# Gated cross-attention block on one core: ScalarE's exponentials ahead of two copies, the second norm's scaling two slots sooner

## The reference

```python
x = x + tanh(g_xattn) * attention(layernorm(x), ctx, ctx)    # x, ctx: (32, 256, 256) f32, 16 heads of 16
x = x + tanh(g_ffn)   * ffn(layernorm(x))                    # 256 -> 768 -> 256, quantised weights and activations
# attention: q, k, v = y @ W.T + b; rotary embedding of q and k;
#   scores = q k^T / 4, -1e9 where |i - j| > 50; softmax; weighted sum of v; @ Wo.T + bo
# ffn: q(x) -> up, gate; gate * sigmoid(gate); * up; @ w_down.T, each rounded with one scale for the whole tensor
```

## Time and profile before

| | |
|---|---|
| median of 3 runs | 1364.79 us (1361.7 to 1365.65) |
| profiled execution | 1366.92 us, of which the trace spans 1365.2 us |
| attention, one unit of the steady part | 22.35 us |
| busy over the span | PE 1198.0 us, DVE 1200.9 us, ACT 830.6 us, POOL 561.2 us |
| granted TensorE clock, steady part | 1.00 |

### The profile page before, as it was taken

How to read it: one execution, slowest core, us unless ns; L and a number is a source line. 1 busy time by engine, 2 the same in 40 slices (tenths; PEclk the granted TensorE clock), 3 DMA queues, 4 the chain that set the end, 5 groups by cost and what they waited for, 6 DMA issues and landing times. The chain is left out here.

```text
span 1365.2 us, 27834 instructions
## 1 busy us (share of the span) xinstructions
PE 1198.0 (88%) x8995; PEld 790.7 (58%) x8995; DVE 1200.9 (88%) x3603; ACT 830.6 (61%) x1336; POOL 561.2 (41%) x1357
## 2 busy tenths in 40 slices
PE   5789898989898989888898759998999799968998
PEld 3457676767666666666665434443433334427887
DVE  3789999999999999999998749997999989988886
ACT  3256666666666666666665436664677599983332
POOL 1177777777777777787877510000000000000000
PEclk9699999999999999999999769998999999988999
DMA  2636454545545554546462302223455455646765
GB/s 78 170 106 190 132 172 143 162 145 159 159 145 148 156 165 140 172 133 172 137 183 87 102 8 93 116 92 127 163 183 185 157 191 197 199 165 205 244 222 169
DMA packets 132369, 207.27 MB, mean 152 GB/s; under 512 B 11159, under 2 KB 97050, under 8 KB 126106
## 3 DMA queue, kind: packets, MB, share of 16 engines
q1 hardware_dynamic: 132250, 205.86, 47.6%
HBM read 125.60 MB, written 79.69 MB: 150 GB/s over the span
## 5 line engine op out<-in xcount | busy, mean ns | idle before, releaser
L670 DVE CUSTOM_DVE_ANT_0 psum<-psum,band 128x178 f32<-128x178 f32 x1024 | 317.2, 373 | 47.6 <-PE psum L880 47.2
L551 ACT ACTIVATE probs<-psum 128x356 f32<-128x356 f32 x512 | 210.9, 469 | 152.4 <-PE psum L897 152.3
L1090 PE MATMUL psum<-xnT,w_upT 128*128 (+1 forms) x1152 | 261.2, 384 | 18.9 <-DVE maxima L1314 8.8
L485 POOL TENSOR_SCALAR_AFFINE_SELECT probs<-probs 128x154 f32<-128x154 f32 (+1 forms) x512 | 212.2, 431 | 140.8 <-ACT probs L551 138.4
L1090 PEld LDWEIGHTS psum<-xnT,w_upT 128*128 128x128 f16 x1152 | 109.9, 99 | 170.0 <-issue 32.6
L494 POOL TENSOR_SCALAR_AFFINE_SELECT probs<-probs 128x254 f32<-128x254 f32 (+1 forms) x512 | 205.0, 425 | 0.0
L897 PE MATMUL psum<-q_stack,k_stack 98*128 98x178 bf16 x1024 | 133.2, 242 | 35.9 <-ACT probs L551 24.5
L880 PE MATMUL psum<-k_stack,q_stack 96*128 96x178 bf16 x1024 | 136.8, 245 | 24.2 <-DVE smax L670 21.4
L670 DVE DVE_READ_ACCUMULATOR2_ANT smax<- 128x1 f32 x1024 | 142.9, 140 | 0.0
L1690 PE MATMUL psum<-w_downT,xnT 128*128 128x256 f16 x1152 | 128.3, 276 | 15.9 <-DVE xnT L1640 15.9
L1090 PE MATMUL psum<-xnT,w_gateT 128*128 (+1 forms) x576 | 126.5, 383 | 6.9 <-DVE xnT L1163 6.9
(11 more groups left out here) (190 smaller groups left out, 2274.0 us busy)
## 6 DMA issues: line engine op xcount, KB each, us to landing
k_parts_scratch<-k_parts SPq DMA_DIRECT2D x32, 384.0 KB, 2.5
q_parts_scratch<-q_parts SPq DMA_DIRECT2D x32, 384.0 KB, 2.7
k_stack<-k_parts_scratch SPq DMA_DIRECT2D x32, 384.0 KB, 4.1
q_stack<-q_parts_scratch SPq DMA_DIRECT2D x32, 384.0 KB, 4.8
gate_scratch<-g_stage SPq DMA_DIRECT2D x16, 768.0 KB, 3.3
g_in<-gate_scratch SPq DMA_DIRECT2D x16, 768.0 KB, 4.6
sig_scratch<-w_gateT SPq DMA_DIRECT2D x32, 384.0 KB, 2.3
sig_again<-sig_scratch SPq DMA_DIRECT2D x32, 384.0 KB, 3.4
```

What stands on the lines that cost most here:

```text
L485: nc.gpsimd.affine_select(out=t[:, :, 0:n], in_=t[:, :, 0:n], pattern=[[0, 2], [1, n]], compare_op=ALU.is_ge, fill=0.0, base=WINDOW - off, ...
L551: nc.scalar.activation(ring_tile(probs, b, pair, c)[:].rearrange("p e j -> p (e j)"), scoreT_bank[c][:, 0:2 * SPAN], ACT.Exp, scale=DK ** ...
L670: ins = nc.vector.tensor_tensor_reduce(out=mine, in0=mine, in1=keep["band"][:, t, :], scale=1.0, scalar=-3e38, op0=ALU.add, op1=ALU.max, a ...
L1090: last = nc.tensor.matmul(bank[:], weights[wp][:, c * I + f * P:c * I + (f + 1) * P], x_parts[:, c, bass.ds(j * (2 * TILE) + xp * TILE, TI ...
```

## The change

- **ScalarE.** In slot 4, q's high part and V's copy move from ahead of the exponentials to behind them, in the order high part of q, middle part of k, V's copy. The second norm's scaling of b4 moves from the end of slot 4 to slot 2, ahead of that slot's exponentials.
- **GpSimd.** The second norm's factors move from slot 2 to slot 1, ahead of slot 1's cuts.
- **VectorE.** q's remainder in slot 5 moves from ahead of the maxima to behind them, just ahead of k's low part.

No instruction is added or removed. TensorE's and SP's orders are as before.

```diff
@@ GpSimd, steps
+                    if slot == 1:
+                        scale_of(Batch(rnd, unit, 4), moments2_taken, scale2_steps, scale2_ready, moments2, scale2_small, scale2)
                     if slot == 2:
-                        scale_of(Batch(rnd, unit, 4), moments2_taken, scale2_steps, scale2_ready, moments2, scale2_small, scale2)
                         rotate(Batch(rnd, unit, 0), "k")
@@ ScalarE, steps, ahead of the slot's exponentials
                     if slot == 4:
                         shift_copy(b2, 1)
                         copy_outT(b3, 1)
-                        high(b0, "q")
-                        if b0.n == 0:
-                            act.wait_ge(consts_set, NBUF)
-                        if b0.real:
-                            copy_out(b0, projected["v"], 1, 1, bank_b[:].rearrange("p (h d) -> p h d", d=DK),
-                                     v_heads(b0.buf)[:, :, 0:DK], v_copied, [(weighted, b0.before(NBUF), PAIRS, PAIRS)])
+                    if slot == 2 and b4.real:
+                        reached(act, x2_transposed, b4.before(1), 1, 1)
+                        normalise(b4, x2[b4.buf], xn2, scale2, scale2_ready, x2_normed)
@@ ScalarE, steps, behind the slot's exponentials
                     if slot == 4:
+                        high(b0, "q")
                         middle(b0, "k")
+                        if b0.n == 0:
+                            act.wait_ge(consts_set, NBUF)
+                        if b0.real:
+                            copy_out(b0, projected["v"], 1, 1, bank_b[:].rearrange("p (h d) -> p h d", d=DK),
+                                     v_heads(b0.buf)[:, :, 0:DK], v_copied, [(weighted, b0.before(NBUF), PAIRS, PAIRS)])
                     if slot == 5:
                         middle(b0, "q")
-                    if slot == 4 and b4.real:
-                        reached(act, x2_transposed, b4.before(1), 1, 1)
-                        normalise(b4, x2[b4.buf], xn2, scale2, scale2_ready, x2_normed)
@@ VectorE, steps
-                    if slot == 5:
-                        remainder(b0, "q")
...
                     if slot == 5:
+                        remainder(b0, "q")
                         low(b0, "k")
```

## The result

The changed kernel takes 1350.3 us (median of 3 runs, 1349.2 to 1352.1) against 1364.8 us: a ratio of 0.990, with a 95% interval of 0.988 to 0.993. Measured again later beside the first experiments it took 1354.3 us (6 runs, 1347.1 to 1358.6) against 1364.7: 0.992 (0.990 to 0.994). The forecast was 1343 us with a range of 1328 to 1359 us. So the sign and the range held, and the saving of 14.5 or 10.4 us is about half to two thirds of the 21.4 us that I had worked out.

The account below looks back on a forecast made before the run. VectorE and TensorE, both almost full, were taken to bound the kernel, with VectorE's run setting the unit's end. 29 x 0.78 = 22.6 us less 1.2 gave 21.4 us saved: 1343 us from 1364.8, range 1328 to 1359.

Parts of the forecast that it names:

- What sets the unit: VectorE's gapless run from slot 0 to slot 6's maxima gates the unit; removing waits of 0.15, 0.22 and 0.41 us saves 0.78.
- TensorE's 0.81 us wait for exponentials: TensorE's slot 5 wait for slot 4's exponentials would go; not itself the gain, but makes room for it.
- VectorE's idle time ahead of slot 0: VectorE's wait for scores before the next slot 0's maxima would shrink from 1.04 to 0.63 us.
- rival B: VectorE's back-to-back subtractions collide with GpSimd's slot 4 cuts, leaving about 0.3 us per unit, 1354 to 1358 us; chance 0.12.
- this term: q's remainder on VectorE, moved beside slot 4's cuts: kept at 0.94 us, no gain; its spread makes 0.3 to 1.0 us per unit.
- The two engines' collision: By the port-lock rule each VectorE subtraction can wait for a whole GpSimd cut; durations read as near 0.69 or 0.94 us.
- Rival C: Slower: late second norm factors hold up slot 2's exponentials; at 3.2 us delay, 0.9 us more per unit, 1370 us; chance 0.07.
- V's copy and slot 3's cuts: V's copy, 1.1 us later, is just hidden before slot 6's transposes; slot 3's cuts end at 523.04, when weighing's second pair can start.
- The second norm's cover: In slot 2, ScalarE's scaling ends at 515.2, leaving 1.1 us before the exponentials; no cost while that holds.
- SP's queue: Later q parts change nothing on SP: store and stack loads stay as far from next slot 3, to 0.3 us.
- The term of 22.6 us: The steady units' saving: 29 units at 0.78 us each.
- The last units: Scaling in slot 2 delays slot 3's turned-weight copies, about 0.9 and 0.3 us; cost taken as 1.2 us, bounds 0 to 3.

Follow-up runs that it names:

- exponentials alone: Only ScalarE's new slot 4 order and VectorE's remainder move, second norm left as before the change, against the kernel before: 1358.2 us, ratio 0.995.
- norm alone: Only the second norm moved (GpSimd's factors to slot 1, ScalarE's scaling to slot 2), against the kernel before: 1351.0 us, ratio 0.991.
- remainder ahead: Changed kernel with q's remainder put back ahead of slot 5's maxima on VectorE: 1364.0 us, ratio 1.000 to the kernel before.
- small cuts: Changed kernel with GpSimd's cuts of slots 4 to 6 covering only 2 columns of each head: 1342.6 us, ratio 0.983 to the kernel before.
- the repair: Changed kernel with the second norm placed as before the change in units that start no new batch: 1347.8 us, ratio 0.987 to the kernel before.
- the cleaner pair: Changed kernel with the shift rows' load ahead of q's stack loads, without and with the second norm late in the last units: 1342.3 against 1335.8 us.

## Why the prediction was right, and where it was off

- **What sets the unit.** Right. The undisturbed unit is 0.84 us shorter, where the waits on the chain gave 0.78 us. The chain in three parts, as medians between the starts at 300 to 700 us:

  | us | before | exponentials alone | norm alone | changed | remainder ahead | small cuts |
  |---|---|---|---|---|---|---|
  | VectorE, slot 0's to slot 6's maxima | 16.20 | 16.06 | 15.94 | 15.89 | 16.31 | 15.59 |
  | slot 6's maxima to b3's projection (L855) | 2.32 | 2.31 | 1.82 | 1.79 | 1.79 | 1.81 |
  | projection to the next slot 0's maxima | 3.85 | 3.84 | 3.85 | 3.84 | 3.84 | 3.84 |

  The first was to lose 0.15 + 0.22 = 0.37 us and lost 0.31, the second 0.41 and lost 0.53, the third nothing. Each part of the change moved the line that its wait stood in. TensorE's 0.81 us wait for exponentials was, as stated, not the gain: taking it away alone gave 0.14 us, and leaving it in gave 0.75 us.
- **VectorE's idle time ahead of slot 0** was to be 0.63 us and is 0.25 us. Of the difference 0.26 us is VectorE's work behind slot 6's maxima, above all q's low part, which went from 0.69 to 0.87 us and which the prediction did not name; 0.12 us is the 0.53 in place of 0.41. Ahead of slot 6's maxima k's low part went from 0.68 to 0.89 us, as rival B had it, while q's remainder fell from a mean of 0.93 to 0.75. The prediction had kept this term at nil, and it came out near nil because the two cancel: that is luck. The small cuts price the collisions at 0.27 us per unit.
- **The two engines' collision.** The Trainium skill (SBUF — State Buffer, "Who interferes with whom") says that a VectorE instruction with two SBUF inputs contends with a GpSimd instruction that reads SBUF, for a pair of ports that is an exclusive lock. The rows agree that they contend: with the cuts small, all three subtractions take 0.69 us, and beside them a pair of cuts takes 1.13 us in place of 0.69. They do not show a subtraction that waits out a whole cut of 0.3 to 0.4 us: the three took 0.06 to 0.20 us more in the mean. Nor are there two durations only, as the prediction read from its rows: k's remainder takes 0.83 us in every unit of 300 to 700 us, before and after.
- **Rival C's price** was added up wrong: 0.9 us more in 29 units is 26 us and gives about 1390 us, not 1370. Made real it took 1396.1 us.
- **V's copy and slot 3's cuts** come nearly in time: TensorE waits 0.3 us for each.
- **The second norm's cover** was put at 1.1 us; 1.23 us are left. Behind the cuts it is overrun.
- **SP's queue: the step that failed.** I followed the stores and the stack loads to slot 3 and found them as far off as before. I left out the last load of the same queue, b1's shift rows, which slot 2 needs sooner than slot 3 needs the stacks. The term of 22.6 us was therefore counted as if every unit were undisturbed: the changed kernel's 28 units saved 22.3 us in one profile and 17.4 in the other. Most of the step between these two is the first unit's granted clock (0.87 in the second), which no term had. Issued sooner, these rows give back 8 to 12 us in the measured time, but only 3.1 and 4.4 us of it are seen in the units where TensorE waited for them; where the rest lies in the unprofiled runs is open.
- **The last units** were priced at 1.2 us with a bound of 3; the first profile gives 3.2 us in the last stretch, and the wait for slot 1's cuts costs 3.4 to 3.6 us by the rows; the repair gave 6.5 us in the cleaner pair, where 1.7 of the 7.0 us of the last stretch are the granted clock. The mechanism was rival C's, GpSimd waiting ahead of cuts that did not need it, in the only units where VectorE's statistics stand behind something else. I had looked at ScalarE's queue there and not at GpSimd's.
- **The start** had no term. The trace of the changed kernel is 2.1 us later at unit 3. Of this 1.8 us is q's first projection, which took 3.78 us against 1.99. The second profile of the same kernel has 1.99 us there, and the kernel before with the shift rows sooner has 3.78, so that is not the change.

## What to carry over

When a schedule is tight, price a move by the chain that gates the period, not by the longest wait: here the 0.8 us wait was worth 0.14 us and the smaller ones 0.75. Before shortening a period, list every transfer with a deadline in the next one, the last of each queue first: its slack is what is spent. And check a move that adds a wait in the filling and draining units apart, where what it waits for stands elsewhere.

## What the runs showed of the hardware

Subtractions of 128x512 with both inputs in SBUF took 0.69 us on VectorE with GpSimd's masks small. With the full ones the three followed here took 0.75 to 0.93 us in the mean where they lay beside them. Moving one of them moved the price to its neighbours: 0.93, 0.68 and 0.69 us became 0.75, 0.89 and 0.87.

Two loads of 4 KB issued last, behind six of 128 to 384 KB, ended TensorE's wait 5.5 us after the second was issued, in the one long unit shown. q's stack loads landed in 5.3 us in the median there, and in 4.1 us where the small loads stood ahead of them.

A wait of TensorE can cost more than itself. With the factors behind the cuts it stood about 1.5 us in a unit; in 14 of 28 units the granted clock then fell, to 0.93 over the unit, and the unit took 24.3 us instead of 22.69.
